# Graph-network chain on one core: heads' queries and keys stacked through a main-memory buffer, heads' row tiles one by one, a new stage order

## The reference, cut to what matters

```python
# x [16, 512, 256], adj [16, 512, 512] (0 or 1, float32 arithmetic throughout)
x = layernorm(x + L0(x, adj))   # graph attention: softmax over neighbours, then elu
x = layernorm(x + L1(x, adj))   # three times: graph attention, layernorm, feed-forward 256-1024-256 (gelu), layernorm
x = layernorm(x + L2(x, adj))   # graph attention, only the 16 largest weights of each row kept
x = layernorm(x + L3(x, adj))   # masked attention with 8 heads of 32 channels
# L3:
q, k, v = heads(x @ Wq), heads(x @ Wk), heads(x @ Wv)        # [16, 8, 512, 32]
scores = einsum('bhnd,bhmd->bhnm', q, k) / sqrt(32)
attn = softmax(where(adj, scores, -inf))
out = relu(merge(einsum('bhnm,bhmd->bhnd', attn, v))) @ Wo
```

## Time and profile before

| | |
|---|---|
| time, median of 3 runs | 4443.77 us (4441.03 to 4455.85) |
| time of the profiled execution | 4446.48 us |
| its span, first to last instruction | 4444.8 us |
| TensorE busy | 3643.0 us (82%) |
| VectorE, ScalarE, GpSimd busy | 2395.6, 2041.9, 700.2 us |
| idle time of TensorE in the span | 801.8 us |

### The profile page before, as it was taken

How to read it: one execution, slowest core, us unless ns; L and a number is a source line. 1 busy time by engine, 2 the same in 40 slices (tenths; PEclk the granted TensorE clock), 3 DMA queues, 4 the chain that set the end, 5 groups by cost and what they waited for, 6 DMA issues and landing times.

```text
span 4444.8 us, 61125 instructions
## 1 busy us (share of the span) xinstructions
PE 3643.0 (82%) x18304; PEld 2854.6 (64%) x18304; DVE 2395.6 (54%) x6607; ACT 2041.9 (46%) x4233; POOL 700.2 (16%) x684
## 2 busy tenths in 40 slices
PE   2778979788788978889788798878978888897866
PEld 1666766667566666666666666666766666676643
DVE  2355555646556565456645555565556546555543
ACT  1244535445444544535454454544535454454523
POOL 0211111111121212111111121212112111121110
PEclk9889989899898989889898899989989898899976
DMA  4001102020110201102020110201102020110202
GB/s 112 1 1 38 35 12 58 4 51 22 28 45 1 62 10 45 28 13 57 3 56 18 29 43 2 66 6 44 29 17 56 1 56 17 34 39 9 52 3 62
DMA packets 140683, 140.73 MB, mean 32 GB/s; under 512 B 42528, under 2 KB 106656, under 8 KB 140320
## 3 DMA queue, kind: packets, MB, share of 16 engines
q1 hardware_dynamic: 131872, 127.97, 11.3%
q0 software_dynamic: 8448, 8.39, 1.3%
HBM read 35.55 MB, written 8.39 MB: 10 GB/s over the span
## 4 chain that ended last, share of the span: by engine, by line
PE 52%; DVE 17%; issue 11%; SPq 9%; ACT 7%; POOL 2%; DMA 1%; DVEq 1%; ACTq 0%; POOLq 0%
PE work L1108 13%; PE acc L1122 12%; PE acc L1086 5%; SPq L429 4%; SPq L431 4%; PE work L1031 4%; PE work L1156 3%; PE acc L1174 3%; PE work L1134 2%; PE work L1145 2%; DVE stats L672 2%; PE work L1044 2%; PE work L1072 2%; PE acc L1207 2%; POOL rstd L481 2%
## 5 line engine op out<-in xcount | busy, mean ns | idle before, releaser
L1108 PE MATMUL work<-XT,w_sb 128*128 128x256 f32 x3072 | 765.3, 397 | 91.8 <-ACT XT L917 33.5
L481 POOL TENSOR_TENSOR rstd<-var_eps,minus_half 128x2 f32<-128x2 f32 x320 | 227.1, 710 | 3533.2 <-DVE var_eps L681 3531.0
L1122 PE MATMUL acc<-w_sb,gT 128*128 128x256 f32 x3072 | 736.5, 388 | 0.0
L1108 PEld LDWEIGHTS work<-XT,w_sb 128*128 128x128 f32 x3072 | 589.0, 199 | 212.2 <-issue 40.8
L1122 PEld LDWEIGHTS acc<-w_sb,gT 128*128 128x128 f32 x3072 | 597.1, 196 | 105.7 <-issue 18.6
L927 ACT ACTIVATE gT<-work,b_sb 128x256 f32<-128x256 f32 x768 | 356.1, 474 | 460.6 <-PE work L1108 456.2
L1145 PE MATMUL work<-k,q 128*128 128x512 f32 x512 | 234.7, 517 | 175.4 <-DMA k<-pos 106.7
L1072 PE MATMUL work<-ident,T 128*128 128x128 f32 x1280 | 209.8, 314 | 195.9 <-DVE T L651 164.7
L1086 PE MATMUL acc<-X,PT 128*128 128x256 f32 x1536 | 348.5, 382 | 0.0
L1072 PEld LDWEIGHTS work<-ident,T 128*128 128x128 f32 x1280 | 175.1, 163 | 226.4 <-DVE T L651 176.3
L1086 PEld LDWEIGHTS acc<-X,PT 128*128 128x128 f32 x1536 | 291.4, 192 | 39.0
(11 more groups left out here) (126 smaller groups left out, 5738.1 us busy)
## 6 DMA issues: line engine op xcount, KB each, us to landing
k<-X SPq DMA_DIRECT2D x512, 64.0 KB, 2.0
k<-pos SPq DMA_DIRECT2D x512, 64.0 KB, 2.0
q<-R SPq DMA_DIRECT2D x512, 32.0 KB, 1.8
q<-HX SPq DMA_DIRECT2D x512, 32.0 KB, 1.9
HX<-in_x SPq DMA_DIRECT2D x16, 512.0 KB, 3.9
pos<-in_adj POOLq DMA_DIRECT2D x16, 512.0 KB, 5.5
out<-X SPq DMA_DIRECT2D x32, 256.0 KB, 2.2
w_sb<-in_L_gnn_W SPq DMA_DIRECT2D x6, 1024.0 KB, 9.0
```

What stands on the lines that cost most here:

```text
L481: pool.tensor_tensor(rstd[s][:, half_rows(half)], var_eps[s][:, half_rows(half)], minus_half[:], ALU.pow)\
L1108: last = pe.matmul(u.bank[:, 0:HN], w1_sb[:, l, c, f * P:(f + 1) * P], XT[s][:, c, half * HN:(half + 1) * HN], start=(c == 0), stop=(c == ...
L1122: last = pe.matmul(acc[s][half][:, i, :], gT[:, f, i * P:(i + 1) * P], w2_sb[:, l, f, :], start=(f == 0 and i == 0), stop=(f == FC - 1), s ...
```

## The change

Three things.

1. *The stack.* `q_hi`, `q_lo`, `k_hi` and `k_lo` of a chunk are first written to two buffers in main memory (`strips`) that have the stacked order, by 8 transfers of 256 KB a chunk (stage `wr{m}`); then a unit's q4 is read by one transfer of 128 KB, and a head's k4 by one of 256 KB for both halves (`st{u}`). k4 has four places, one for each head of a chunk. The projections are by chunk (`qk0`, `qk1`) and no longer `q` and `k`.
2. *Row tiles one by one.* `sc`, `ex` and `uT` are stages of one row tile (k = 0 to 31) and no longer of a unit with two. The uses of the work banks are numbered scores k0, k1, then k2, pT k0, k3, pT k1 and so on, so that the scores of a slot have one bank and the transposes the other.
3. *`HALF`* is a new list.

```diff
     HALF = [
...
-        ("ending", "L1.2", "f211 f212"), ("middle", "L0", "sum0 norm0"), ("ending", "L1.2", "f213"),
-        ("middle", "L0", "sum1"), ("ending", "L1.2", "xsum1"), ("middle", "L0", "norm1"),
-        ("middle", "L1.0", "xT0 xT1"), ("ending", "L1.2", "xnorm1"), ("middle", "L1.0", "s"),
-        ("ending", "L1", "norm1"), ("ending", "L2", "xT0"), ("middle", "L1.0", "bc zs0 mx0 zs1"),
-        ("ending", "L2", "v0 xT1 v1"), ("middle", "L1.0", "exp0"), ("ending", "L2", "bc zs0"),
-        ("middle", "L1.0", "mx1"), ("ending", "L2", "mx0 zs1"), ("middle", "L1.0", "exp1 pT0"),
-        ("ending", "L2", "exp0 mx1 tk0 kp0 tk1 exp1 kp1 pT0"), ("middle", "L1.0", "pT1 pT2"),
-        ("ending", "L2", "tk2 kp2 pT1"), ("middle", "L1.0", "pT3"), ("ending", "L2", "tk3"),
-        ("middle", "L1.0", "agg0"), ("ending", "L2", "kp3 pT2"), ("middle", "L1.0", "agg1 sum0 norm0"),
-        ("ending", "L2", "pT3 agg0"), ("middle", "L1.0", "sum1 norm1 hT0"), ("ending", "L2", "agg1 sum0"),
-        ("middle", "L1.0", "hT1 f100"), ("ending", "L2", "norm0 sum1 norm1"), ("ending", "L3", "xT0"),
-        ("middle", "L1.0", "f101 f102 f103 f200"), ("ending", "L3", "v0"), ("middle", "L1.0", "f110"),
-        ("ending", "L3", "xT1"), ("middle", "L1.0", "f201 f111"), ("ending", "L3", "v1 q"),
-        ("middle", "L1.0", "f202"), ("ending", "L3", "k st0"), ("middle", "L1.0", "f112 f203 f113"),
-        ("ending", "L3", "sc0 st1 ex0 st2"), ("middle", "L1.0", "xsum0 xnorm0 f210"),
...
+        ("middle", "L0", "norm1"), ("middle", "L1.0", "xT0"),
+        ("ending", "L1.2", "xnorm0"), ("ending", "L1", "norm0"), ("ending", "L1.2", "f210 f211 f212 f213"),
+        ("middle", "L1.0", "xT1"), ("ending", "L1.2", "xsum1"), ("middle", "L1.0", "s"),
+        ("ending", "L1.2", "xnorm1"), ("middle", "L1.0", "bc zs0 mx0"), ("ending", "L1", "norm1"),
+        ("middle", "L1.0", "zs1"), ("ending", "L2", "xT0"), ("middle", "L1.0", "exp0 mx1"),
+        ("ending", "L2", "v0 xT1"), ("middle", "L1.0", "exp1 pT0"), ("ending", "L2", "v1"),
+        ("middle", "L1.0", "pT1"), ("ending", "L2", "bc zs0 mx0"),
+        ("middle", "L1.0", "pT2 pT3 agg0 agg1 sum0 norm0 sum1 norm1 hT0"), ("ending", "L2", "zs1 exp0"),
+        ("middle", "L1.0", "hT1 f100"), ("ending", "L2", "mx1 tk0 kp0 tk1"),
+        ("middle", "L1.0", "f101 f102 f103 f200"), ("ending", "L2", "exp1 kp1"), ("middle", "L1.0", "f110"),
+        ("ending", "L2", "pT0"), ("middle", "L1.0", "f201"), ("ending", "L2", "tk2"),
+        ("middle", "L1.0", "f111 f202 f112"), ("ending", "L2", "kp2 pT1"), ("middle", "L1.0", "f203"),
+        ("ending", "L2", "tk3"), ("middle", "L1.0", "f113"), ("ending", "L2", "kp3 pT2 pT3"),
...
+        ("ending", "L3", "xT0 xT1"), ("middle", "L1.0", "xsum1 xnorm1"), ("middle", "L1.1", "xT0"),
+        ("ending", "L3", "qk0"), ("middle", "L1.1", "xT1"), ("ending", "L3", "wr0"),
+        ("middle", "L1.1", "s bc zs0"), ("ending", "L3", "v0 st0"), ("middle", "L1.1", "mx0"),
+        ("ending", "L3", "st1"), ("middle", "L1.1", "zs1"), ("ending", "L3", "st2 v1"),
+        ("middle", "L1.1", "exp0 mx1"), ("ending", "L3", "qk1 wr1 sc0"), ("middle", "L1.1", "exp1"),
+        ("ending", "L3", "ex0"), ("middle", "L1.1", "pT0"), ("ending", "L3", "sc1 ex1 sc2 uT0"),
...
+        ("ending", "L3", "st5 ex6"), ("middle", "L1.1", "sum0"), ("ending", "L3", "sc7 uT5 ex7 sc8"),
+        ("middle", "L1.1", "norm0"), ("ending", "L3", "uT6 st6 ex8 sc9 uT7 ex9 sc10 pv0 uT8 st7"),
...
+        ("ending", "L3", "uT12 st9 ex14 sc15 uT13 ex15 sc16"), ("middle", "L1.1", "f110"),
+        ("ending", "L3", "uT14 st10 ex16 sc17"), ("middle", "L1.1", "f201"), ("ending", "L3", "uT15 ex17"),
+        ("middle", "L1.1", "f111 f202"), ("ending", "L3", "sc18 pv1 uT16 st11 ex18 rr0 sc19 uT17"),
...
-        k4 = sb("k4", [P, RING, N], F32R)
+        k4 = sb("k4", [P, HPC, N], F32R)
...
+        strips = {name: nc.dram_tensor(f"{name}_strips", [SLOTS, DC, HPC, 4, DK, N], F32).ap() for name in "qk"}
...
+        uses += [("scores k0", 1), ("scores k1", 1)]
+        for k in range(NK):
+            uses += [(f"scores k{k + 2}", 1)] if k + 2 < NK else []
+            uses += [(f"pT k{k}", 1)]
...
+            def write(m):
+                def stage(s, it, key):
+                    for name, parts, (hi, lo), written in (("q", (0, 0, 1, 1), (q_hi, q_lo), q_written[m]),
+                                                           ("k", (0, 1, 0, 1), (k_hi, k_lo), k_written[m])):
+                        there = strips[name][s, m]
+                        sp.wait_ge(split.sems[s], split.value(it, name, m))
+                        for strip in range(4):
+                            if parts[strip] == 0:
+                                sp.dma_start(there[:, strip], hi[s][:, m, :]).then_inc(written.sems[s], 16)
...
+                        sp.wait_ge(use.evacuated, use.turn + 1)
+                        for strip in range(4):
+                            if parts[strip] == 1:
+                                sp.dma_start(there[:, strip], lo[s][:, m, :]).then_inc(written.sems[s], 16)
...
             def stack(u):
-                    for part, (q_part, k_part) in enumerate(parts):
-                        at = slice(part * DK, (part + 1) * DK)
-                        sp.dma_start(q4[at, u % RING, :].bitcast(F32), q_part[s][rows, m, cols])\
-                            .then_inc(stacked[u % RING].sems[s], 16)
-                        sp.dma_start(k4[at, u % RING, :].bitcast(F32), k_part[s][rows, m, :])\
-                            .then_inc(stacked[u % RING].sems[s], 16)
+                    if half == 0 and r == 0:
+                        sp.wait_ge(q_written[m].sems[s], q_written[m].value(it, "L3", 4 * 16 - 1))
+                    if u >= RING:
+                        wait_multiplied(s, it, u - RING)
+                    sp.dma_start(q4[:, u % RING, :].bitcast(F32),
+                                 strips["q"][s, m, r].rearrange("strip d n -> (strip d) n")[:, cols])\
+                        .then_inc(q_stacked[u % RING].sems[s], 16)
+                    if half == 1:
+                        return
+                    if r == 0:
+                        sp.wait_ge(k_written[m].sems[s], k_written[m].value(it, "L3", 4 * 16 - 1))
+                    if m > 0:
+                        wait_multiplied(s, it, u - HPC)
+                    sp.dma_start(k4[:, r, :].bitcast(F32), strips["k"][s, m, r].rearrange("strip d n -> (strip d) n"))\
+                        .then_inc(k_stacked[r].sems[s], 16)
```

More of the change, by code:

```diff
@@ L291, in build @@
         neg_row_ready = signal("neg_row_ready", [(k, 2) for k in ATT])
-        min_done = signal("min_done", [(f"u{u}", 1) for u in range(NU)])
         edge_step = signal("edge_step", [("L0", 2)])
@@ L425, in stage @@
-                    rows, cols = slice(r * DK, (r + 1) * DK), slice(half * HN, (half + 1) * HN)
-                    parts = ((q_hi, k_hi), (q_hi, k_lo), (q_lo, k_hi), (q_lo, k_lo))
-                    for part, (q_part, k_part) in enumerate(parts):
-                        at = slice(part * DK, (part + 1) * DK)
-                        sp.dma_start(q4[at, u % RING, :].bitcast(F32), q_part[s][rows, m, cols])\
-                            .then_inc(stacked[u % RING].sems[s], 16)
-                        sp.dma_start(k4[at, u % RING, :].bitcast(F32), k_part[s][rows, m, :])\
-                            .then_inc(stacked[u % RING].sems[s], 16)
+                    cols = slice(half * HN, (half + 1) * HN)
@@ L443, in _ @@
             stages = {"load": load_next, "store0": store(0), "store1": store(1)}
-            stages |= {f"st{u}": stack(u) for u in range(NU)}
+            stages |= {f"st{u}": stack(u) for u in range(NU)} | {f"wr{m}": write(m) for m in range(DC)}
             walk(0, opening, stages)
@@ L761, in x_norm, with lower_parts @@
                 return stage
-            def lower_parts(name, hi, lo, scale):
+            def lower_parts(m):
                 def stage(s, it, key):
-                    for c in range(DC):
-                        u = Use(s, it, f"{name} L3", c)
-                        dve.wait_ge(split.sems[s], split.value(it, name, c))
-                        dve.scalar_tensor_tensor(lo[s][:, c, :].bitcast(F32R), u.bank[:], scale, hi[s][:, c, :],
+                    for name, hi, lo, scale in (("q", q_hi, q_lo, -float(DK) ** -0.5), ("k", k_hi, k_lo, 1.0)):
+                        u = Use(s, it, f"{name} L3", m)
+                        dve.wait_ge(split.sems[s], split.value(it, name, m))
+                        dve.scalar_tensor_tensor(lo[s][:, m, :].bitcast(F32R), u.bank[:], scale, hi[s][:, m, :],
@@ L785, in unit_transposed, with head_transposed @@
-            def unit_transposed(u):
+                    use = Use(s, it, f"scores k{k}")
+                    dve.wait_ge(use.filled, use.turn)
+                    hold(dve)
+                    dve.tensor_tensor_reduce(score_tile(s, u, i), use.bank[:], pos0[s][:, half * HT + i, :], 1.0, HIGHEST,
```

(26 more changed lines are left out.)

133 lines of the change are left out of this document (68 added, 65 removed), and 70 rows, old and new, of the table HALF.

## The result

The changed kernel takes 4688.6 us (median of 4 runs, 4684.19 to 4701.91), the kernel before 4445.7 us beside it (4 runs, 4441.03 to 4455.85): a ratio of 1.0548, interval 1.0519 to 1.0577. It is slower by 243 us, where 4368 us was forecast, 78 us less than the profiled execution before. The profiled execution took 4701.91 us, its span is 4700.3 us.

The account below looks back on a forecast made before the run. TensorE, busy 82% of the span, was taken as the bound, with 38 us of waits a pass to move. Terms gave -4.2 us a pass, -63 over fifteen, -15 in the last: 4446 - 78 = 4368 us, range 4280 to 4465.

Parts of the forecast that it names:

- L2's pT0 to pT3 behind `keep`: First transposes of the top-16 layer: TensorE's wait for VectorE's `keep` goes, hidden by feed-forward stages, -9.4 us a pass.
- L1.0's xT1: L1.0's second transpose, now behind f210 to f213, 14 us after its aggregation in place of 8: -2.5 us a pass.
- L2's v0 and what stood there before: Top-16 layer's v0 waits for VectorE's copy, starting 10.9 us after xT1 where it was 6.3: +4.6 us a pass.
- L1.0's hT0, hT1, f100: End of L1.0's attention: hT1 waits about 3 us for norm1, with a short wait at hT0: +0.6 us a pass.
- f213 to the first score: From L1.0's last f213 to the first score: short waits for copies that f1 stages covered before, +1.0 us a pass.
- stack (sc0, sc1, sc2, sc6): Heads' first scores, stack through main memory: sc0 waits 2.5 us where head units waited 4.6: -2.0 us a pass.
- row tiles, table loads: Heads' single tiles and L1.1's feed-forward: bank waits, VectorE's statistics, 20 table loads for 14: +3.5 us a pass.
- the queue: SyncE's 40 issues a batch, 26 us for 82, lie beside TensorE's work in a steady pass but for the first units.
- the clock: Mean granted clock of 0.90, taken as equal before and after the change.
- rival 4: Slower: ScalarE paces L1.1's feed-forward through table loads, a pass costs 11 us in place of 3, 4488 us; chance 0.18.
- over 8 us of DMA at sc0: Sign of a wrong forecast: the heads' first score waits this long for DMA, memory being slower than both bounds.
- The last pass: Tail, one batch alone: waits for the stack go but for the first, short bank waits replace them: -15 us, once.

Follow-up runs that it names:

- e1: Changed kernel with the main-memory buffers ordered row, strip, column, so a write has 128 outermost steps in place of 4; 4174.6 us, ratio 0.9396 to the kernel before.
- e5: Changed kernel with each head in its main-memory buffers cut into two blocks of 16 rows, so a write has 8 outermost steps in place of 4; 4336.8 us.
- e3: Changed kernel with the second chunk's writes (`wr1`) moved in the list from before sc0 to behind st5; 4548.9 us.
- e2: Changed kernel without main-memory buffers: new list, row tiles and k4 places stay, stacks copied SBUF to SBUF; 4200.7 us, ratio 0.9454 to the kernel before.
- e4: Kernel before, its list and tiles kept, with the stacks by way of main memory in the changed kernel's layout; 4921.5 us.
- e6: Kernel before, its list and tiles kept, with the stacks by way of main memory in e1's layout; 4469.7 us.

## Why the prediction was wrong

Steady passes follow each other at 265.1 us before, 281.3 in the changed kernel and 248.6 in e1 (the starts of passes 1 and 15 in the three traces, over 14). The forecast for a pass, -4.2 us, stands against +16.2 and -16.5. Term by term, waits of TensorE in a steady pass, mean of 13:

| term | forecast | changed kernel | e1 |
|---|---|---|---|
| L2's pT0 to pT3 behind `keep` | -9.4 | -9.0 | -9.0 |
| L1.0's xT1 | -2.5 | -2.5 | -2.5 |
| L2's v0 and what stood there before | +4.6 | +4.6 | +4.4 |
| L1.0's hT0, hT1, f100 | +0.6 | +1.0 | +0.9 |
| f213 to the first score | +1.0 | +2.4 | +2.4 |
| stack (sc0, sc1, sc2, sc6) | -2.0 | **+23.2** | -4.5 |
| row tiles, table loads | +3.5 | -0.9 | 0.0 |
| other places | 0 | -0.7 | -0.6 |
| sum of waits | -4.2 | +18.1 | -8.9 |
| TensorE's work | 0 | -2.1 | -7.8 |

**The step that failed is the stack by way of main memory**, where the prediction put 256 KB at 1.05 to 1.7 us, let sc0 wait "0 to 4.5 us, and I take the middle, 2.5", and had "the second set of writes ... done before sc6". (Its own bounds, 10 to 14 us beside 11 of TensorE's work, give 0 to 3 us and not 4.5; that slip is small beside the rest.) Measured are 2.6 us for 256 KB, 13.2 us at sc0 and 14.25 at sc6: +23.2 us a pass for -2.0. Two things were wrong in it, and they worked against each other. Full-share rates of 244 GB/s and less were too slow: the changed kernel's own writes would make 392 on all engines, 0.67 us for 256 KB, an estimate that e1's window of 390 GB/s bears out. And the writes ran on a quarter of the engines, which no row of before shows, since none of its transfers has 4 outermost steps; e1, e5 and the shares of 0.26 and 0.52 show that it is this. Both bounds were prices of another shape of transfer, so the true value lay outside of them. The rest of the chain was right: in e1 sc0 stands 11.4 us after the end of qk0 (2622.7 to 2634.1 in TensorE's timeline), and k4 has landed before it, some 10 us after that end, the prediction's lower bound. In the changed kernel eight writes of 2.6 us are 20.6 us, k4's read goes out 24.3 us after the first, and sc0 starts 26.3 us after the end of qk0 (2636.7 to 2663.0); TensorE's other work takes 14.3 of them, more than in e1, part of it at the lower clock.

**A second part of the same step** was the queue. In a steady pass SyncE's time was taken as free "but for the first units", at 0.64 us an issue. With the writes slow, k's writes kept SyncE 2.45 us each in the mean, and unit 3's reads came behind them at 2676.8 and 2679.2. Most of sc6's wait lies behind that: the read of k4 then needed 9.1 us to land in place of 2.8, so by the trace it stood behind the writes on the DMA engines too. The prediction named what is queued behind a waiting instruction for other engines and not here. e3 shows that it is the place behind the writes: with `wr1` later, sc6 waits nothing and sc12 does. How the wait divides between SyncE's queue and the DMA engines is read from one pass of the trace; no run separates them.

**The second mis-sized term was hidden by the first**: the clock, "taken as equal", and with it TensorE's work. In e1 a pass has 7.8 us less of work for the same matmuls, 118.8 us over the span (3643.0 to 3524.2). Two groups of the lines view show it, first of before, then of e1, the matmul of weights and v in the heads (busy, mean ns):

```profile
L1174 PE MATMUL acc<-PT,V 128*32 128x256 f32 x2048 | 173.4, 497 | 0.0
```

```profile
L1222 PE MATMUL acc<-PT,V 128*32 128x256 f32 x2048 | 140.3, 420 | 3.5 <-DVE PT L828 3.1
```

The granted clock of a whole pass is 0.90 before and 0.94 in e1; in the heads' stretch (windows of e1, 2625 to 2690) it is 1.00, where before (2780 to 2840) it was 0.89. In a steady pass of e1 the heads' scores, transposes and products wait for nothing longer than 0.8 us, and nothing in that stretch is at the lower of the two levels (0.50 of full speed, 1.2 GHz). In the changed kernel the lower level is there again: the windows from 2656 to 2664, with the stop before sc0 in them, are granted 0.53 and 0.50, and the score that ends the stop takes 0.79 us where the same one of e1 takes 0.54. But the clock was at 0.50 already from 2640 to 2644, ahead of the stop and with TensorE busy 3.74 of 4 us, so the stop is not the only cause. The changed kernel and e1 have the same order of work and differ in the layout alone: with 27 us more of stops a pass, TensorE's work is 5.7 us longer (89.6 over the span). The other 2.1 of the 7.8 us stand between before and the changed kernel, which differ in order and in stops; what makes them was not separated.

**The tiles** were dear in the forecast by 3.5 us and cost nothing. Bank waits are there as forecast, about 6 us a pass on L1192 and L1204 together, but the list of before had as many, spread over rows smaller than the two that were counted against them (about 7.7 us with the waits on `head_min`, 0.8 of them in fact a wait for the sixth unit's stack). The gelu banks wait 0.7 us a pass: rival 4 named the right end of the scale for another reason, and its own mechanism is refuted. Its price from twenty table loads, +11 us, is not there.

**Right** were the gain at top-16, L1.0's xT1, the sum of the stages before L2's v0 (10.9 us after xT1, measured 2848.7 - 2837.8 = 10.9 in the changed kernel), about 3 us before hT1 (3.6), and the 20 table loads, which the page's instruction count bears out. The text's own sign for a wrong forecast, "over 8 us of DMA at sc0", is what came.

**The last pass** was to gain 15 us. It takes 457.6 us before, 491.2 in the changed kernel and 417.0 in e1: 34 lost where the writes have nothing to hide behind, 41 gained where they are quick. In the tail of e1 the 16 units follow at 3.8 us in the mean, before at 5.2 (5.1 for the one of the earlier trace rows); 4.4 was forecast.

The sum closes: 14 distances of 16.2 us are +227, the last pass +34, the opening -4: 257 for the 255.5 us between the two spans. In e1 14 x -16.5 - 41 - 2 = -274, and the spans differ by 274.0.

## What to carry to other kernels

Before a transfer is priced from others, compare its shape with theirs on both sides: the number of outermost steps decides how many DMA engines it gets, and a flat DMA share of 0.25 or 0.5 in the windows is that and not the memory. Eight writes and the read-back need some 11 us of cover even when all engines work (in e1 8.0 to the read's issue and 2.7 to its landing), and what is queued behind the writes, on the issuing engine and on the DMA engines, needs it too. Judge a new order without its slowest part (e1 beside the changed kernel): the list and the row tiles here were worth over 5% (e2), and the change as a whole measured 5.5% slower.

## What the runs showed of the hardware

- The rate of a write into main memory goes with its outermost steps: 102 GB/s and a share of 0.26 with 4, 201 and 0.52 with 8, 273 to 390 and 0.77 to 1.04 with 128, the highest with reads among the writes, for the same bytes from the same buffers.
- SyncE's issue of a 256 KB write takes 0.3 to 0.65 us in e1's first set, up to 1.7 in its second, and with 4 steps 2.45 us in the mean once four such writes are ahead of it, about the 2.6 us of one write: the issues then go at the pace of the transfers.
- A read behind slow writes lands late: unit 3's k4 in the changed kernel 9.1 us after its issue, where the median is 2.8.
- In the changed kernel, e3, e4 and e5 (4 or 8 steps) the page gives no landing time for the writes, in e1 and e6 (128) it does (2.7 to 3.6 us): a missing figure there is worth a look at SyncE's timeline.
- The same 18304 matmuls and transposes took 3643.0, 3613.8 and 3524.2 us of TensorE's time before, in the changed kernel and in e1, at a mean granted clock of 0.896, 0.882 and 0.930; the last two have the same order of work.
